# Attention of 64-row halves: score and row products of neighbouring heads in two halves of the array, row sums divided by way of DRAM

## The chip, the cores and the metric

The kernel runs on one core of a Trainium2 chip. The metric is the device time of one execution in microseconds. The profiler's trace of one execution gives the rows that are quoted below. Engines are named as in the profile: PE is TensorE (PEld its weight loads), DVE VectorE, ACT ScalarE, POOL GpSimd, SP SyncE, which here only issues DMAs.

## What is computed

The kernel is a two-layer network on a (2, 1024, 256) input. Each layer holds one causal softmax attention with 16 heads of 16 channels; between and behind them stand expert layers, a frequency mixing and a recurrent layer, which the change does not touch. The attention, cut from the reference:

```python
q = (x @ wq).reshape(b, t, HEADS, HEAD_DIM)     # HEADS 16, HEAD_DIM 16, t 1024
k = (x @ wk).reshape(b, t, HEADS, HEAD_DIM)
v = (x @ wv).reshape(b, t, HEADS, HEAD_DIM)
scores = jnp.einsum('bqhd,bkhd->bhqk', q, k)
mask = jnp.arange(t)[:, None] < jnp.arange(t)[None, :]
scores = jnp.where(mask, -jnp.inf, scores)
attn = jax.nn.softmax(scores / np.sqrt(HEAD_DIM), axis=-1)
ctx = jnp.einsum('bhqk,bkhd->bqhd', attn, v).reshape(b, t, EMB)
return ctx @ wo + bo
```

## The kernel before

`attention` (L343) runs twice, the first time from 39.3 us, the second from 1717 us of the span. It takes the 16 heads of both batch entries in 8 groups of four heads (GH = 4), each group in one **turn**. A turn n works on two groups at once. For group m = n + 1 it makes the **row products** (`first`, L519): 48 matmuls that multiply 128 queries by up to 512 keys, so that VectorE (`maximum`, L672) can take each query's largest score. For group n it makes the **scores** (`scores`, L543), this time with keys in rows and 512 queries in columns; two more contraction rows carry the negated maximum, so that ScalarE (`probabilities`, L633) can go straight from PSUM through the exponential into `a_prob`. Then `values` (L559) multiplies the probabilities by the values, four heads side by side in four 32-column parts of the array. Queries and keys are split in a high and a low part in fp32r, and three of the four products of parts are stacked in the contraction, which is why one head pair takes 96 rows (98 with the maximum).

The function `turn` (L293) writes the order by hand, and all engines follow the same list. A turn has 12 **steps** (STEPS): step i takes one block of 128 keys for one half of the queries, and has four scores, one for each head. Steps 0 to 3 and 8 to 11 lie on the causal diagonal. Their scores are 512, 384, 256 and 128 columns wide, and POOL first cuts a triangle out of the probabilities (L475); steps 4 to 7 are 512 wide and are not cut. `FIRSTS_AFTER` says how many row products follow each score, and the values of step i - 1 come after the four scores of step i. `SMALL` puts one small piece at the end of a step: a projection of queries and keys (`qk`, two a turn, behind steps 3 and 4), one of values (`v`, two a turn), the transposed maxima (`max`, L527), and the division by the row sums (`sums` L568 and `spread` L578 on PE, `reciprocals` L701 and `divide` L706 on DVE), twice a turn. The last turn, the closing one, has no row products and has the output projections (`out`, L591) instead.

Eight PSUM banks hold all this: three for row products (FR = 3), three for scores, one shared by the small pieces (SB = 1), one for the values' sums. An instruction waits for a semaphore count: score t waits until the exponential of score t - SR is done, with SR the number of score banks; a row product waits for the maximum that frees its bank. PE takes its instructions in order, so all that stands behind a waiting matmul waits with it.

```python
if t >= SR:
    pe.wait_ge(s["b_exp"], t - SR + 1)                 # scores, L543
if j == 0 and n * HALF + h:
    pe.wait_ge(s["o_cp"], n * HALF + h)                # values, L559
```

The queries and keys of a head pair reach their rows by DMAs that SP issues (`place_keys`, `place_queries`; for the very first half ScalarE issues them, L620). Each layer's semaphores are cleared by `end_layer`, which also holds a barrier.

## Time and profile before

| | us |
|---|---|
| median of 3 runs (lowest, highest) | 2411.98 (2408.28, 2419.59) |
| profiled execution, its own time | 2414.42 |
| span of that execution | 2412.6 |
| first attention, from the first projection to the last addition | 39.3 to 451.9 |
| second attention | 1717.0 to 2130.9 |
| PE busy over the span | 2034.7 (84%) |
| DVE busy, ACT busy | 1599.6, 856.7 |
| mean granted TensorE clock, share of full speed | 0.908 |

The profiled execution lies 2.4 us above the median. The two attentions are 34% of the span. The stretches of the first one stand in the rows below: start of the projections, row products of the first group alone, first turn, and so on to the closing turn. Busy time is a union of the records of an engine; TensorE's matmuls are pipelined, so that its busy share says only that it was never without one. What one matmul costs its successor is read from start to start.

### The profile page before, as it was taken

The numbers are of one execution on the slowest core, as the hardware profiler recorded it, in microseconds if no ns is written. First come the engines' busy times: TensorE is split into PE (matmuls) and PEld (weight loads), VectorE is DVE, ScalarE is ACT, GpSimd is POOL, SyncE is SP. The second block draws the span as 40 slices with busy tenths as digits, with TensorE's granted clock in tenths as the row PEclk, the third lists the DMA queues.
The fourth block names the chain that finished last, engine by engine and source line by source line (L and its number), as shares of the span: only waits on it lengthen the run. The fifth ranks groups of instructions, "written<-read, shape, count | busy, mean of one in ns | idle before, by whom it ended". The sixth has DMA issues, their size and how long they took to land. (4 is left out here: it accounts for less than half of the span.)

```text
span 2412.6 us, 32196 instructions
## 1 busy us (share of the span) xinstructions
PE 2034.7 (84%) x11288; PEld 1386.3 (57%) x11288; DVE 1599.6 (66%) x3514; ACT 856.7 (36%) x1599; POOL 446.7 (19%) x324
## 2 busy tenths in 40 slices
PE   7899999699999989757766385646689999999998
PEld 4466665388888867334433242323356666469997
DVE  3677773254544355779999999995567777246775
ACT  2255554122223222431112111111335555435775
POOL 0011110423333030001001100110001010105775
PEclk9699999799999999878887698868879999989999
DMA  4111110211110010200000000000121211018886
GB/s 158 42 36 38 44 35 10 83 57 53 52 52 17 0 53 1 86 1 9 9 3 7 18 9 9 0 0 18 36 47 35 47 36 29 9 37 255 235 234 125
DMA packets 52448, 122.19 MB, mean 51 GB/s; under 512 B 14224, under 2 KB 25232, under 8 KB 49488
## 3 DMA queue, kind: packets, MB, share of 16 engines
q1 hardware_dynamic: 42704, 107.40, 14.9%
q0 software_dynamic: 8832, 12.16, 2.9%
q8 instruction: 81, 1.33, 0.2%
q10 hardware_dynamic: 768, 0.79, 0.1%
q14 instruction: 63, 0.52, 0.1%
HBM read 84.09 MB, written 10.52 MB: 39 GB/s over the span
## 5 line engine op out<-in xcount | busy, mean ns | idle before, releaser
L672 DVE CUSTOM_DVE_ANT_0 a_junk<-pair,a_mask 128x512 f32<-128x512 f32 (+3 forms) x768 | 394.2, 551 | 188.1 <-PE pair L519 184.5
L633 ACT ACTIVATE a_prob<-pair 128x512 f32<-128x512 f32 (+3 forms) x768 | 329.0, 496 | 306.5 <-PE pair L543 303.4
L543 PE MATMUL pair<-a_qx,a_kx 98*128 98x512 f32 (+3 forms) x768 | 266.0, 393 | 6.8 <-ACT a_prob L633 6.7
L519 PE MATMUL pair<-a_kx,a_qx 96*128 96x512 f32 (+3 forms) x768 | 246.2, 391 | 22.7 <-DMA a_qx<-a_comp 17.9
L475 POOL TENSOR_SCALAR_AFFINE_SELECT a_prob<-a_prob 128x512 f32<-128x512 f32 x128 | 81.2, 635 | 700.2 <-ACT a_prob L633 700.2
L903 DVE TENSOR_TENSOR m_h<-pair,m_g 128x512 f32<-128x512 f32 x96 | 66.3, 691 | 211.3 <-PE pair L726 210.2
L1285 PE MATMUL pair<-h_stream,r_w_kz 128*128 128x512 f32 x192 | 103.9, 695 | 118.5 <-DVE r_region L1691 113.3
L724 PE MATMUL pair<-m_x_hi,m_w_lo 128*128 128x512 f32 x448 | 178.1, 398 | 26.5 <-POOL m_w_lo L788 24.4
L519 PEld LDWEIGHTS pair<-a_kx,a_qx 96*128 96x128 f32 x768 | 150.6, 204 | 70.4 <-DVE a_mx_raw L672 28.2
L543 PEld LDWEIGHTS pair<-a_qx,a_kx 98*128 98x128 f32 x768 | 143.0, 193 | 74.4 <-ACT a_prob L633 39.3
L725 PE MATMUL pair<-m_x_hi,m_w_hi 128*128 128x512 f32 x448 | 176.8, 395 | 0.0
L726 PE MATMUL pair<-m_x_lo,m_w_hi 128*128 128x512 f32 x448 | 176.8, 395 | 0.0
L559 PE MATMUL pair<-a_prob,a_v 128*32 128x512 f32 (+3 forms) x1536 | 165.4, 503 | 1.5 <-POOL a_prob L475 1.2
L864 ACT ACTIVATE m_g<-pair 128x512 f32<-128x512 f32 x96 | 57.4, 598 | 285.8 <-PE pair L726 285.8
L1329 PE MATMUL pair<-r_hq,r_spread 128*128 128x256 f32 x320 | 86.3, 437 | 84.1 <-DVE r_region L1820 71.4
L1285 PEld LDWEIGHTS pair<-h_stream,r_w_kz 128*128 128x128 f32 x192 | 41.1, 224 | 172.7 <-DVE r_region L1691 116.5
L1705 DVE TENSOR_TENSOR r_region<-r_region 128x1536 f32<-128x1536 f32 (+7 forms) x160 | 129.9, 853 | 2.7
L1345 PE MATMUL pair<-r_u,r_w_ring 128*128 128x512 f32 x256 | 124.0, 630 | 4.8 <-DVE x_stream L1807 4.8
L1329 PEld LDWEIGHTS pair<-r_hq,r_spread 128*128 128x128 f32 x320 | 70.5, 223 | 99.8 <-DVE r_region L1820 74.2
L881 DVE TENSOR_TENSOR m_h_lo<-m_h,m_h_hi 128x512 fp32r<-128x512 f32 x112 | 124.6, 1113 | 0.3
L1555 POOL TENSOR_TENSOR r_y<-r_region 128x512 f32<-128x512 f32 x16 | 20.3, 1269 | 519.7 <-DVE r_region L1820 497.8
L724 PEld LDWEIGHTS pair<-m_x_hi,m_w_lo 128*128 128x128 f32 x448 | 85.5, 191 | 49.8 <-POOL m_w_lo L788 21.5
(305 smaller groups left out, 4254.7 us busy)
## 6 DMA issues: line engine op xcount, KB each, us to landing
mx_raw<-in_L_ffn_experts SPq DMA_DIRECT2D x69, 512.0 KB, 4.9
m_raw<-in_L_cond_experts SPq DMA_DIRECT2D x18, 1024.0 KB, 4.8
a_kx<-a_comp SPq DMA_DIRECT2D x96, 128.0 KB, 2.4
a_qx<-a_comp SPq DMA_DIRECT2D x360, 32.0 KB, 2.0
r_w_ring<-in_r_q_w SPq DMA_DIRECT2D x8, 512.0 KB, 3.9
m_raw<-in_L_cond_experts SPq DMA_DIRECT2D x6, 512.0 KB, 3.4
token_rows<-mx_h_rows SPq DMA_DIRECT2D x2, 1040.0 KB, 8.1
x_stream<-in_x SPq DMA_DIRECT2D x1, 2048.0 KB, 10.6
```

What stands on the lines that cost most here:

```text
L519: nc.tensor.matmul(first_bank[t % FR][:, 0:c1 - c0], qx[0:PRODUCT, m % 2, a, i * P:(i + 1) * P], kx[0:PRODUCT, m % 3, a // 2, c0:c1], star ...
L543: nc.tensor.matmul(score_bank[t % SR][:, q0:TT], kx[0:ROWS, n % 3, a // 2, j * P:(j + 1) * P], qx[0:ROWS, n % 2, a, h * TT + q0:(h + 1) * ...
L559: last = nc.tensor.matmul(value_bank[r, q0:TT], v_sb[:, n % 2, j, r], prob[:, i % RING, a, q0:TT], start=j == 0, stop=j == 4 * h + 3)
L633: nc.scalar.activation(prob[:, i % RING, a, q0:TT], score_bank[t % SR][:, q0:TT], ACT.Exp, scale=SCALE).then_inc(s["b_exp"], 1)
L672: nc.vector.tensor_tensor_reduce(out=junk[:, t % 2, 0:cols], in0=first_bank[t % FR][:, 0:cols], in1=mask[:, m0:m0 + cols], scale=1.0, scal ...
L724: nc.tensor.matmul(out, w_lo, x_hi, start=first, stop=False)
L725: nc.tensor.matmul(out, w_hi, x_hi, start=False, stop=False)
L726: return nc.tensor.matmul(out, w_hi, x_lo, start=False, stop=last)
L881: nc.vector.tensor_tensor(h_lo[:, n % RING, :], h_sb[:, n % 2, :], h_hi[:, n % RING, :].bitcast(F32), ALU.subtract).then_inc(q["lo"], 1)
L1285: last = nc.tensor.matmul(bank, w_kz[:, k, part * DI + m * P:part * DI + (m + 1) * P], seq(c.h, b)[:, k, half(h)], start=k == 0, stop=k == ...
L1329: last = nc.tensor.matmul(spread_bank(v, h)[:, t * QW_:(t + 1) * QW_], spread[:, 2 * h + t, m, :], hq[:, b, v, :], start=True, stop=True)
L1705: did(tt(pr[:, i, :, :, :], right[:, 3 * i:3 * i + 2, :].unsqueeze(1).broadcast_to([P, 3, 2, n]), left.rearrange("p (j q) n -> p q j n", j ...
```

## The change

**Row halves.** A head now takes 48 contraction rows (50 with the maximum) and even heads lie in rows 0 to 63 of the array, odd heads in rows 64 to 127. Row product and score of a slot lie in different halves (`FIRST` now runs over heads 1, 0, 3, 2), so that one can run beside the other. **Banks.** Row products have four PSUM banks, scores two. The maximum writes its masked scores back in place, not to a junk tile. **Order.** One row product follows each score; the values of step i - 1 come after the second score of step i, no longer after the fourth. **Projections.** ScalarE copies the high part twice more (`twin`), so that one DMA places all three parts of a head: 4 DMAs in place of 12 for a half of the queries, and 4 in place of 6 for the keys. Values are projected for two groups at once, once a turn. ScalarE takes over from VectorE the copies of values and of maxima. **Division.** For groups 0 to 6 the PE pieces `sums` and `spread` fall away. The sums go to DRAM, come back as 64 rows, are inverted, go to DRAM again and come back spread over 32 rows for each head; one 1024-column product on DVE divides. The last group keeps the old way. **Layer end.** One more `end_layer` stands ahead of the last branch.

On PE, at step 5 of a middle turn (the L543/L585 rows are scores, L519/L560 row products, L559/L601 values, L494/L533 projections). Before, from the last score of step 4 on:

```order
L543 MATMUL pair<-a_qx,a_kx 128x512 [waits a0_b_exp]
L559 MATMUL pair<-a_prob,a_v 32x128 [waits a0_b_cut,a0_b_exp]
L559 MATMUL pair<-a_prob,a_v 32x128 x3
L494 MATMUL pair<-h_stream,w_qkv 128x512 [waits a0_used]
L494 MATMUL pair<-h_stream,w_qkv 128x512
L543 MATMUL pair<-a_qx,a_kx 128x512 [waits a0_b_exp]
L519 MATMUL pair<-a_kx,a_qx 128x384 [waits a0_a_max]
L543 MATMUL pair<-a_qx,a_kx 128x512 [waits a0_b_exp] x2
L519 MATMUL pair<-a_kx,a_qx 128x512 [waits a0_a_max] x3
L543 MATMUL pair<-a_qx,a_kx 128x512 [waits a0_b_exp]
L559 MATMUL pair<-a_prob,a_v 32x512 [waits a0_o_cp,a0_b_exp]
L559 MATMUL pair<-a_prob,a_v 32x512 x3
```

And now, from the last two scores of step 4 on:

```order
L585 MATMUL pair<-a_qx,a_kx 128x512 [waits a0_b_exp]
L560 MATMUL pair<-a_kx,a_qx 128x512 [waits a0_a_max]
L585 MATMUL pair<-a_qx,a_kx 128x512 [waits a0_b_exp]
L560 MATMUL pair<-a_kx,a_qx 128x512 [waits a0_a_max]
L533 MATMUL pair<-h_stream,w_qkv 128x512 [waits a0_used]
L533 MATMUL pair<-h_stream,w_qkv 128x512
L585 MATMUL pair<-a_qx,a_kx 128x512 [waits a0_b_exp]
L560 MATMUL pair<-a_kx,a_qx 128x128 [waits a0_a_max]
L585 MATMUL pair<-a_qx,a_kx 128x512 [waits a0_b_exp]
L560 MATMUL pair<-a_kx,a_qx 128x128 [waits a0_a_max]
L601 MATMUL pair<-a_prob,a_v 32x512 [waits a0_o_cp,a0_b_exp]
L601 MATMUL pair<-a_prob,a_v 32x512 x3
```

The values of step 4 (the row that waits for `o_cp`) stood behind four scores of step 5 and now stand behind two, and each score waits for the exponential two scores back, not three.

On ACT, at the same place. Before, with the projections' high part (L609), the exponentials (L633) and the copy of the results (L640):

```order
L633 ACTIVATE a_prob<-pair 128x128 [waits a0_b_mm] x3
L609 ACTIVATE a_comp<-pair 128x512 [waits a0_q_in0,a0_q_in1,a0_k_in,a0_proj]
L633 ACTIVATE a_prob<-pair 128x512 [waits a0_b_mm,a0_pv]
L633 ACTIVATE a_prob<-pair 128x512 [waits a0_b_mm] x3
L609 ACTIVATE a_comp<-pair 128x512 [waits a0_proj]
L633 ACTIVATE a_prob<-pair 128x512 [waits a0_b_mm,a0_pv]
L640 ACTIVATE a_o_raw<-pair 128x512 [waits a0_used,a0_pv]
L633 ACTIVATE a_prob<-pair 128x512 [waits a0_b_mm] x3
```

And now, with the high part (L653), the new copies (L655), the exponentials (L690) and the copy of the results (L695):

```order
L690 ACTIVATE a_prob<-pair 128x128 [waits a0_b_mm] x3
L653 ACTIVATE a_comp<-pair 128x512 [waits a0_q_in0,a0_q_in1,a0_k_in,a0_proj]
L655 ACTIVATE a_comp<-a_comp 128x2x512 [waits a0_hi]
L690 ACTIVATE a_prob<-pair 128x512 [waits a0_b_mm,a0_pv]
L690 ACTIVATE a_prob<-pair 128x512 [waits a0_b_mm] x3
L653 ACTIVATE a_comp<-pair 128x512 [waits a0_proj]
L655 ACTIVATE a_comp<-a_comp 128x2x512 [waits a0_hi]
L690 ACTIVATE a_prob<-pair 128x512 [waits a0_b_mm,a0_pv]
L695 ACTIVATE a_o_all<-pair 128x512 [waits a0_pv]
L690 ACTIVATE a_prob<-pair 128x512 [waits a0_b_mm] x3
```

Behind each high part one copy has come in, ahead of the four exponentials of the step.

The diff, cut to its core:

```diff
-PRODUCT = 3 * 2 * HD
+PRODUCT = 3 * HD
...
-FIRST = [(a, i, c_) for part in (range(4), range(4, QT)) for a in range(GH) for i in part for c_ in range(i // 4 + 1)]
+FIRST = [(a, i, c_) for part in (range(4), range(4, QT)) for i in part for c_ in range(i // 4 + 1) for a in (1, 0, 3, 2)]
...
-FR, SB = 3, 1
+FR, SB = 4, 1
...
+SMALL = (("max", 0, 1), None, None, ("qk", 2, 0), ("qk", 2, 1), ("max", 1, 0), ("v", 0, 0), None, None, None, None, None)
...
+NORM = {2: 0, 3: 1, 6: 2, 7: 3, 9: 4}
+NORM_LAST = {1: 0, 2: 1, 4: 2, 5: 3, 6: 4, 8: 5}
...
-            if (i, a) == (0, 1) and n:
-                order += [("values", n - 1, NS - 1), ("copy", n - 1, 1)]
-            for f in range(found, found if closing else min(NF, found + FIRSTS_AFTER[i][a])):
-                order.append(("first", m, f))
+            if (i, a) == (2, 0) and n > 1:
+                order.append(("norm", n - 2, 5))
+            if not closing:
+                order.append(("first", m, found))
                 found += 1
...
+            if a == 1 and i:
+                order.append(("values", n, i - 1))
+            elif a == 1 and n:
+                order += [("values", n - 1, NS - 1), ("copy", n - 1, 1)]
             if (i, a) == (5, 0):
                 order.append(("copy", n, 0))
-        if i:
-            order.append(("values", n, i - 1))
...
+        def rows_of(a, n):
+            return slice(a % 2 * 64, a % 2 * 64 + n)
...
+                    for a in range(GH):
+                        rows = slice(64 + a * HD, 64 + a * HD + HD)
+                        sp.dma_start(kx[rows_of(a, PRODUCT), m % 3, a // 2, :].bitcast(F32), comp[rows, 0:3, :].bitcast(F32))\
+                            .then_inc(s["k_in"], 16)
...
+                    if step == 0:
+                        sp.wait_ge(s["o_cp"], (n + 1) * HALF)
+                        sp.dma_start(totals[n, :, :], o_all[HD:P:SLOT, group, :].rearrange("p h t -> p (h t)"))\
+                            .then_inc(s["n_out"], 16)
+                    elif step == 1:
+                        sp.wait_ge(s["n_out"], (n + 1) * 16)
...
+                        sp.dma_start(total[:, :, :], totals[n, :, :].rearrange("a (p c) -> p a c", p=64)).then_inc(s["n_in"], 16)
...
+                    r = rows_of(a, PRODUCT)
+                    nc.tensor.matmul(first_bank[t % FR][:, 0:c1 - c0], qx[r, m % 3, a // 2, i * P:(i + 1) * P],
+                                     kx[r, m % 3, a // 2, c0:c1], start=True, stop=True).then_inc(s["a_mm"], 1)
...
+                    r = rows_of(a, ROWS)
+                    nc.tensor.matmul(score_bank[t % SR][:, q0:TT], kx[r, n % 3, a // 2, j * P:(j + 1) * P],
+                                     qx[r, n % 3, a // 2, h * TT + q0:(h + 1) * TT], start=True, stop=True)\
                         .then_inc(s["b_mm"], 1)
...
                     nc.scalar.activation(comp[:, 0, half(h)], bank_of("qk", m, h), ACT.Copy).then_inc(s["hi"], 1)
+                    act.wait_ge(s["hi"], m * HALF + h + 1)
+                    nc.scalar.activation(comp[:, 2:4, half(h)], comp[:, 0:1, half(h)].bitcast(F32).broadcast_to([P, 2, TT]), ACT.Copy)\
+                        .then_inc(s["twin"], 1)
...
+                    elif step == 5:
+                        dve.wait_ge(s["n_wide"], (n + 1) * GH * 16)
+                        tile = o_all[:, n * HALF:(n + 1) * HALF, :].rearrange("p h t -> p (h t)")
+                        nc.vector.tensor_tensor(tile, tile, factor[:, :], ALU.mult).then_inc(s["n_done"], 1)
...
         recurrent(c, A)
+        c.end_layer()
```

## Rows read from the trace of the kernel before

**Rows 1.** the page: busy time and share of each engine; granted TensorE clock in 40 slices

```profile
PE 2034.7 (84%) x11288; PEld 1386.3 (57%) x11288; DVE 1599.6 (66%) x3514; ACT 856.7 (36%) x1599; POOL 446.7 (19%) x324
...
PEclk9699999799999999878887698868879999989999
```

**Rows 2.** stretches of the first attention; the first row names the columns

```profile
core 0: us, PE busy (x) PEld busy (x) DVE busy (x) ACT busy (x) POOL busy (x), PEclk, DMA share, GB/s
39.30:57.90 18.60, 10.53 (x41) 6.71 (x41) 5.88 (x8) 3.75 (x4) 4.50 (x6) 0.82 0.45 103
57.90:89.50 31.60, 27.81 (x60) 14.70 (x61) 24.79 (x98) 4.13 (x4) 0.00 (x0) 0.63 0.15 35
89.50:137.70 48.20, 42.62 (x274) 26.43 (x272) 30.14 (x114) 22.30 (x51) 5.08 (x8) 0.85 0.18 41
137.70:178.80 41.10, 41.10 (x325) 26.27 (x321) 29.64 (x112) 22.27 (x52) 5.08 (x8) 1.00 0.18 41
343.20:381.60 38.40, 37.96 (x317) 24.64 (x313) 28.37 (x110) 21.40 (x50) 5.08 (x8) 1.00 0.10 27
381.60:451.90 70.30, 62.49 (x344) 29.98 (x340) 10.39 (x18) 21.40 (x51) 5.08 (x8) 0.93 0.00 1
```

**Rows 3.** groups of TensorE by shape, one middle turn (178.75 to 219.98 us)

```profile
L543 PE MATMUL pair<-a_qx,a_kx 98*128 98x512 f32 x24 | 9.8, 456 | 0.0
L503 PE MATMUL pair<-w_qkv,h_stream 128*128 128x128 f32 x32 | 4.1, 281 | 0.0
L494 PE MATMUL pair<-h_stream,w_qkv 128*128 128x512 f32 x8 | 4.0, 618 | 0.0
L578 PE MATMUL pair<-ident,a_o_rcp 128*32 128x128 f32 x68 | 2.4, 273 | 0.0
L568 PE MATMUL pair<-sum_pick,a_o_raw 128*128 128x4 f32 x16 | 2.1, 255 | 0.0
```

**Rows 4.** groups of ScalarE in the same turn

```profile
L633 ACT ACTIVATE a_prob<-pair 128x512 f32<-128x512 f32 x24 | 12.8, 606 | 7.3 <-PE pair L543 7.3
L609 ACT ACTIVATE a_comp<-pair 128x512 fp32r<-128x512 f32 x2 | 1.2, 598 | 3.9 <-PE pair L494 3.9
```

**Rows 5.** order of time in the closing turn (start, duration, idle before)

```profile
408.88 1.06 PE L559 MATMUL pair<-a_prob,a_v 128*32 128x512 f32 x8
409.87 1.05 PE L568 MATMUL pair<-sum_pick,a_o_raw 128*128 128x4 f32 x8
410.79 0.94 PE L543 MATMUL pair<-a_qx,a_kx 98*128 98x512 f32 x3
411.36 2.06 ACT L633 ACTIVATE a_prob<-pair 128x512 f32<-128x512 f32 x4 [1.49 <-PE pair L543]
412.01 0.50 PE L543 MATMUL pair<-a_qx,a_kx 98*128 98x512 f32 x1 [0.28 <-ACT a_prob L633]
412.44 1.06 PE L559 MATMUL pair<-a_prob,a_v 128*32 128x512 f32 x8
```

**Rows 6.** the same view at that turn's end, narrower steps and the cut

```profile
420.97 1.64 ACT L633 ACTIVATE a_prob<-pair 128x384 f32<-128x384 f32 x4 [3.99 <-PE pair L543]
432.19 0.97 ACT L633 ACTIVATE a_prob<-pair 128x128 f32<-128x128 f32 x4 [4.15 <-PE pair L543]
...
433.23 0.63 POOL L475 TENSOR_SCALAR_AFFINE_SELECT a_prob<-a_prob 128x512 f32<-128x512 f32 x1 [4.49 <-ACT a_prob L633]
434.01 0.43 PE L559 MATMUL pair<-a_prob,a_v 128*32 128x128 f32 x8 [0.59 <-POOL a_prob L475]
```

**Rows 7.** groups of the whole span: 1024-column operations between SBUF tiles

```profile
L2270 ACT ACTIVATE mx_w_hi<-mx_raw 128x1024 fp32r<-128x1024 f32 x69 | 70.3, 1052 | 2.7 <-DMA mx_raw<-in_L_ffn_experts 2.7
L1781 DVE TENSOR_TENSOR r_y<-r_y,r_z 128x1024 f32<-128x1024 f32 x8 | 9.8, 1219 | 1.3 <-ACT r_y L1493 1.3
```

**Rows 8.** order of time: the first attention's start; after the one layer end

```profile
47.66 7.64 ACTq L620 DMA_DIRECT2D a_qx<-a_comp  x12
...
966.63 0.10 DVE L1825 MEMSET r_region<- 128x16 f32 x2 [1.35 <-PEq L56]
```

More of the change, by code:

```diff
@@ L310, in turn @@
                 uses = []
+            if a == 1 and i:
+                order.append(("values", n, i - 1))
+            elif a == 1 and n:
+                order += [("values", n - 1, NS - 1), ("copy", n - 1, 1)]
             if (i, a) == (5, 0):
                 order.append(("copy", n, 0))
-        if i:
-            order.append(("values", n, i - 1))
+        norm = (NORM_LAST if closing else NORM).get(i)
+        if n and norm is not None:
+            order.append(("norm", n - 1, norm))
         small = (SMALL_LAST if closing else SMALL)[i]
@@ L317, in turn @@
             what, x, y = small
-            entry = (what, x, y) if what == "out" else (what, n + x, y)
-            if 0 <= entry[1] < NG:
+            if what == "out":
+                entry = (what, x, y)
+            elif what == "v":
+                entry = (what, n // 2 + 1, n % 2)
+            else:
+                entry = (what, n + x, y)
+            if entry[1] < (NG // 2 if what == "v" else NG):
                 order.append(entry)
@@ L414, in place_keys @@
                     sp.wait_ge(s["used"], used("qk", m, 1))
-                    if m >= 3:
+                    sp.wait_ge(s["twin"], (m + 1) * HALF)
+                    if m < 3:
+                        sp.wait_ge(s["ones"], m + 1)
+                    else:
                         sp.wait_ge(s["b_exp"], (m - 2) * NS * GH)
-                    for p in range(PAIRS):
-                        rows = slice(64 + p * 32, 96 + p * 32)
-                        for part, low in enumerate((0, 1, 0)):
-                            sp.dma_start(kx[part * 32:part * 32 + 32, m % 3, p, :].bitcast(F32), comp[rows, low, :].bitcast(F32))\
-                                .then_inc(s["k_in"], 16)
+                    for a in range(GH):
+                        rows = slice(64 + a * HD, 64 + a * HD + HD)
+                        sp.dma_start(kx[rows_of(a, PRODUCT), m % 3, a // 2, :].bitcast(F32), comp[rows, 0:3, :].bitcast(F32))\
+                            .then_inc(s["k_in"], 16)
                 def place_queries(m, h):
@@ L439, in place_maxima @@
                 def place_maxima(m, h):
                     sp.wait_ge(s["used"], used("max", m, h))
[L441 to L442 removed]
+                    for x in range(2):
+                        sp.dma_start(qx[x * 64 + PRODUCT:x * 64 + ROWS, m % 3, :, half(h)].bitcast(F32),
+                                     stage[2 * PAIRS * x:2 * PAIRS * x + 2 * PAIRS, :].bitcast(F32))\
@@ L460, in _ @@
             def _(pool):
-                for a in range(GH):
-                    nc.gpsimd.memset(qx[:, 1, a, :].bitcast(F32), 0.0).then_inc(s["zero1"], 1)
+                for x in range(3):
+                    nc.gpsimd.memset(kx[:, x, :, :].bitcast(F32), 1.0).then_inc(s["ones"], 1)
                 nc.gpsimd.memset(v_sb[:, :, :, :].rearrange("p x t (a s) -> p (x t a) s", s=SLOT)[:, :, HD:HD + 1], 1.0)\
@@ L496, in qk_projection, with v_projection @@
                     last.then_inc(s["proj"], 1)
-                def v_projection(m, v):
-                    bank = take("v", m, v)
+                def v_projection(pair, v):
+                    m = 2 * pair
+                    bank = take("v", pair, v)
                     for t in range(4):
@@ L613, in place_first_queries @@
                         return
[L614 removed]
                     act.wait_ge(s["used"], used("qk", 0, 0))
+                    act.wait_ge(s["twin"], 1)
                     for a in range(GH):
                         rows = slice(a * HD, a * HD + HD)
[L618 to L625 removed]
+                        act.dma_start(qx[rows_of(a, PRODUCT), 0, a // 2, half(0)].bitcast(F32), comp[rows, 1:4, half(0)].bitcast(F32))\
+                            .then_inc(s["q_in0"], 16)
                 def probabilities(n, i, a):
@@ L637, in copy_result @@
                     act.wait_ge(s["pv"], n * NS + (4 if h == 0 else NS))
-                    if n:
-                        act.wait_ge(s["used"], used("spread", n - 1, h))
-                    nc.scalar.activation(o_raw[:, h, :], value_bank, ACT.Copy).then_inc(s["o_cp"], 1)
-                does = {"qk": upper, "q_slots": place_first_queries, "scores": probabilities, "copy": copy_result}
+                    nc.scalar.activation(o_all[:, n * HALF + h, :], value_bank, ACT.Copy).then_inc(s["o_cp"], 1)
+                does = {"qk": upper, "q_slots": place_first_queries, "scores": probabilities, "copy": copy_result,
+                        "v_use": copy_values, "max_use": copy_maxima}
                 for what, *which in ORDER:
@@ L648, in _ @@
             def _(dve):
-                for a in range(GH):
-                    nc.vector.memset(qx[:, 0, a, :].bitcast(F32), 0.0).then_inc(s["zero0"], 1)
                 dve.wait_ge(s["mask"], 16)
```

170 lines of the change are left out of this document (87 added, 83 removed).

## Prediction

> **What bounds the kernel now.** The page comes first: PE is busy 84% of the span, in the attentions 99% [rows 1]. The stretches say more [rows 2]: a middle turn takes 41.1 us and PE is busy in all of it at full clock, while DVE has 29.6 us and ACT 22.3 us of work. The groups of that turn show no idle time ahead of any PE group, and ACT idle for want of scores (7.3 us) and of projections (3.9 us) [rows 3, 4]. So a middle turn is TensorE's time. What that leaves unseen is the latency around ACT, since PE always has something else to do. The closing turn, which has no row products, shows it [rows 5]: the fourth score waits for a bank (idle 0.28, released by ACT).
>
> **TensorE's work after the change.** Three 512-column scores start 0.24 us apart (0.94 [rows 5] less one duration of 0.46 [rows 3], halved). A turn has 24 such scores and 24 narrower ones (by width about 0.12 each), some 8.6 us, and as many row products. If the halves run side by side, half of 17.2 is saved, 8.6. The sums and the spread go (2.1 + 2.4), and half of the value projections (4.1 / 2 = 2.0) [rows 3]. That is 15.1 us, and 26.0 remain of 41.1. The Trainium skill (TensorEngine Tiling (Array Packing), Theoretical Speedup) gives up to 2x for a contraction of 64 or less; no row here shows row halves, and by that rule the saving would be this 8.6. Its section PSUM Bottleneck speaks against the change: tiling speeds up TensorE and not the emptying of PSUM.
>
> **What is late next: the round through ACT with two banks.** Handovers from [rows 5]: a first score starts at 410.79 and its exponential at 411.36, 0.57 later. Four exponentials take 2.06, one 0.61, so each follows the last by 0.48. The waiting score starts at 412.01, 1.22 after the first, and the values 0.43 later; from values to the next PE work it is 0.99 (408.88 to 409.87). The cut comes from [rows 6]: POOL starts 0.07 after the last exponential (its row 432.19 + 0.97 = 433.16), takes 0.63, and the values start at 434.01: 0.85 in all.
>
> Now one step in the new order, from the start of its third score (time 0). A 512-wide step without cut: third exponential 0.57 to 1.18, fourth to 1.66. The first score of the next step needs the third's bank, 1.2; the second needs the fourth's, 1.7. Row products run beside them. The values follow the second: 1.7 + 0.43 + 0.1 for the row product = 2.2, and the next third score starts at 3.2. PE has about 2.0 us of work in it, ACT 1.9. With the cut, the values start at 1.66 + 0.85 = 2.5, the next third score at 3.5. For narrower steps exponentials take 0.37 apart at 384 columns, about 0.27 at 256 and 0.17 at 128 (1.64 and 0.97 for four [rows 6]), and values shrink by 0.21 per 128 columns (1.06 against 0.43 busy [rows 5, 6]): 3.1, 2.6 and 2.1. Without extras a turn is 2 x (3.5 + 3.1 + 2.6 + 2.1) + 4 x 3.2 = 35.4 us.
>
> **The projections inside this round.** The high part and the new copy stand ahead of the exponentials on ACT. Two projections are busy 4.0 us, one 2.0 [rows 3], the high part 0.6 [rows 4], the copy 1.05 (1024 columns [rows 7]). From the third score of step 3: projection 0.6 to 2.6, high part to 3.2, copy to 4.3, two exponentials to 5.35; the third score of step 4 waits for the first of them, 4.9, its fourth exponential ends at 6.5. The second projection goes in at 5.7, ends 7.7, high part 8.3, copy 9.35, exponential 9.9, result copy 10.4. The values of step 4 wait for that result copy (`o_cp`), 10.5, so the third score of step 5 starts at 11.5. Without the projections it is 2.1 + 3.2 = 5.3: +6.2. Value projection behind step 6: 16 matmuls at half of 4.1 less the overlap, +0.9. The result copy at the turn's start +0.3; two copies of the maxima (0.6 each) fit in ACT's idle time. Turn: 35.4 + 6.2 + 0.9 + 0.3 = **42.8 us, 1.7 more than now**. I take this and keep -2 and +2.5 us a turn as bounds: 0.2 us a step if the first score after the values needs less than the 0.57 seen, as much if the row product delays them.
>
> **The other parts.** DVE loses sums, spread product, value and maxima copies and gains one 1024-column product of 1.2 us [rows 7] and a reciprocal, staying under 29.6 us: hidden as long as the turn is over that. In-place masking into PSUM has no row; 0, within 0.06 us of a maximum either way, and only the first 48 maxima feel it. The DRAM trips: five steps on SP and DVE over a turn, the product one turn later still; a DMA issue takes 0.64 us (12 in 7.64 [rows 8]), and a step lasts 2 us or more. SP's queue holds `place_keys` and `place_maxima` behind these waits, needed 6 to 20 us later: 0. If a trip took over 8 us, DVE would stop at its reciprocal with all maxima behind it. Start of an attention: now 18.6 + 31.6 us [rows 2]. The 12 issues on ACT become 4, saving 5 us of the 7.64, and two copies and the values' copies give half back: -2.5. The 48 maxima need 24.8 of 31.6 us; fourth bank and halves give -2.5. Bounds of both together 0 and -9. Turn 6 has no projections: 35.4 + 0.3 + 0.7 (result copy ahead of the values of step 4) = 36.4 against 38.4, -2. Closing turn: the same outputs, one pair of sums and spread fewer, longer rounds: 0, bounds -3 and +3. The layer end: DVE stood 1.35 us at the first one [rows 8]; +1.
>
> **The sum.** Per attention: turns 0 to 5 at +1.7 = +10.2, start -5, turn 6 -2, closing 0: +3. Two attentions and the layer end: 2 x 3.2 + 1 = +7.4 on the profiled 2414.4. The median lies 2.4 lower: 2412 + 7.4 = **2420 us**. The bounds of the turn (12 x -2 and +2.5, not both full with the others) give 2392 to 2450. A measurement of this kernel tells 0.5% (12 us) from no change.
>
> **Rival 1, slower: the clock.** TensorE's granted clock is 1.00 (2.4 GHz) in the middle turns, where PE never pauses, and 0.63 where it waited for DVE between row products [rows 2], that is mostly the 1.2 GHz level. The new turn pauses 17 of 42.8 us, up to 2.5 us at a time around the second projection. The first turn shows the price: granted 0.85, 48.2 against 41.1, +7.1 us [rows 2]. All 12 turns from 0 to 5 at 0.85 give about 12 x 7 = +85 on the 2420: 2505. Above 1 us a turn it decides the sign. Against it: the closing turn pauses too and keeps 0.93. The Trainium skill (TensorE: Matmul & The Clock Gate, psum-queue depth-cycling) tells of a kernel whose short pauses between groups made the clock oscillate, and would side with this rival.
>
> **Rival 2, faster: the round is shorter than its parts.** The score after the values starts loaded (0.3, not 0.57) and the values end 0.3 us sooner for the next score. That is 0.55 us a step, 6.6 a turn: 36.2, 12 x 6.6 = 79 less, 2341. Half of it gives 2380. For it: the 0.57 has a weight load in it. Against: the 1.22 and 0.99 repeat in each step of the closing turn.
>
> **Rival 3: the halves don't run side by side.** Then each row product costs 0.24 us where it stands ahead of values or projection, some 6 places: +1.5 a turn, 2440. That TensorE's 15 us would simply be gained (turn at DVE's 27 to 29 us, near 2260) I hold for hardly possible, since the bank wait is in the code.
>
> **Chances.** Forecast with its own range 0.45, clock 0.27, shorter round 0.23, no concurrency 0.05. Of the forecast 0.08 lies under 2400, 0.20 within 12 us, 0.17 above; rival 2 gives 0.22 to faster. Faster 0.30, same 0.21, slower 0.49. The range runs from 2350, halfway down rival 2, to 2520, just above the clock at 0.85; 0.1 on each side is left out.
>
> **What would show it.** Right: middle turns of 41 to 45 us; PE idle with ACT as the releaser of scores, POOL and ACT of values; the longest hole ahead of the values that follow the second projection; ACT idle still some 15 us a turn. Rival 1: granted clock under 0.95 in turns 1 to 6. Rival 2: turns under 40 us with PE still idle. Rival 3: row product and score starting 0.24 us apart, not together. Wrong altogether: DVE waiting at the reciprocal for a DMA, or DVE busy over 30 us a turn.

## Result and the profile after

The changed kernel takes 2533.4 us (median of 4), the kernel before 2411.4 beside it: ratio 1.050, 95% interval 1.047 to 1.054, 122 us slower. That lies above the range of the prediction, and 113 us above its point.

The profiled execution lasts 2537.9 us against 2412.6. The page's engine shares and granted clock, to be held against [rows 1]:

```profile
PE 2061.3 (81%) x9912; PEld 1246.9 (49%) x9912; DVE 1601.2 (63%) x3414; ACT 921.6 (36%) x1689; POOL 453.7 (18%) x322
...
PEclk9577777889999999888888698778677877698999
```

TensorE has 1376 products fewer and is busy 27 us longer. Both attentions stand mostly at 7 or 8 tenths of the clock where the kernel before had mostly 9. The stretches of the first attention (stretch, length, busy time of each engine with its instructions, granted clock, DMA share and GB/s), answering [rows 2]. The first two are its start, then turn 0, turn 2, four pieces from the start of turn 4 (295.3 to 345.5) on, turn 6 and the closing turn:

```profile
core 0: us, PE busy (x) PEld busy (x) DVE busy (x) ACT busy (x) POOL busy (x), PEclk, DMA share, GB/s
37.50:55.80 18.30, 9.69 (x40) 5.42 (x40) 1.38 (x2) 4.62 (x8) 7.15 (x5) 0.91 0.43 92
55.80:88.40 32.60, 27.92 (x60) 13.82 (x61) 24.53 (x93) 3.89 (x5) 0.00 (x0) 0.57 0.20 38
88.40:141.40 53.00, 44.34 (x217) 17.03 (x216) 29.79 (x106) 26.42 (x56) 4.44 (x7) 0.72 0.24 43
192.90:243.00 50.10, 42.08 (x224) 17.38 (x224) 30.48 (x107) 27.13 (x59) 5.98 (x8) 0.76 0.23 44
295.60:312.60 17.00, 15.08 (x71) 6.15 (x69) 10.83 (x42) 7.48 (x18) 3.89 (x5) 0.50 0.02 4
312.70:322.90 10.20, 6.66 (x38) 2.29 (x36) 4.54 (x14) 6.82 (x11) 0.00 (x0) 1.00 0.11 13
322.90:329.70 6.80, 6.74 (x31) 3.32 (x29) 3.81 (x13) 3.71 (x7) 0.00 (x0) 0.51 0.79 154
329.70:346.80 17.10, 14.20 (x104) 5.91 (x103) 12.24 (x41) 9.89 (x24) 2.54 (x4) 1.00 0.24 56
397.50:440.70 43.20, 36.97 (x200) 13.86 (x200) 28.88 (x106) 23.44 (x53) 5.99 (x8) 0.68 0.09 27
440.70:511.50 70.80, 63.15 (x296) 27.39 (x297) 11.78 (x23) 23.12 (x53) 5.71 (x9) 0.83 0.04 9
```

A middle turn takes 48.9 to 52.2 us where it took 41.1 (the mean of turns 1 to 5 of both attentions is 50.96). Within turn 4 the granted clock goes between its two levels: 0.50 (1.2 GHz) from the turn's start to its fourth step, up to 1.00 (2.4 GHz), once more down, and at 1.00 in steps 7 to 11. The other middle turns have the same 1.00 in steps 7 to 11 and the fall behind it. Measured from the first score of each turn to that of the next, turns 0 to 5 give +55.3 us in the first attention and +54.3 in the second, the two turns 6 give +4.9 and +10.2, all else +0.6. That is the 125.3 us between the two spans. So it is the turns, and nearly nothing but the turns.

What TensorE waits for in turn 2 (busy, mean, then the idle time ahead and who ended it), and the longest hole of turn 4 in the order of time:

```profile
L585 PE MATMUL pair<-a_qx,a_kx 50*128 50x512 f32 (+3 forms) x48 | 20.2, 489 | 3.5 <-ACT a_prob L690 3.5
L601 PE MATMUL pair<-a_prob,a_v 128*32 128x512 f32 (+3 forms) x96 | 13.3, 632 | 4.5 <-ACT a_o_all L695 2.3 <-POOL a_prob L514 1.7 <-ACT a_prob L690 0.5
```

```profile
310.41 3.15 PE L533 MATMUL pair<-h_stream,w_qkv 128*128 128x512 f32 x4
...
316.74 1.98 PE L533 MATMUL pair<-h_stream,w_qkv 128*128 128x512 f32 x4
318.65 0.50 PE L585 MATMUL pair<-a_qx,a_kx 50*128 50x512 f32 x1
318.66 0.32 PE L560 MATMUL pair<-a_kx,a_qx 48*128 48x128 f32 x1
...
321.56 1.07 PE L601 MATMUL pair<-a_prob,a_v 128*32 128x512 f32 x8 [2.30 <-ACT a_o_all L695]
```

L585 is the score, L560 the row product, L601 the values, L533 a projection, L690 the exponential, L695 the result copy, L514 POOL's cut. TensorE had no idle time at all in [rows 3]; now scores wait for exponentials and values for the result copy and the cut. A score and the row product of the other half start 0.01 us apart (318.65, 318.66). The same four projection products last 1.98 us at the upper level of the clock (316.74), 3.15 where the clock rises while they run (310.41, granted 0.62) and 3.78 at the lower level throughout (at 74.56 us).

### The profile page after: what moved, and what is told of

Its sections match the earlier page's. It is cut to its first block and busy times, and to the rows that moved or that the text cites. A ratio compares the mean times of both kernels' runs of the same rounds, so it can differ in the third digit from the quotient of the medians.

```text
span 2537.9 us, 28385 instructions
## 1 busy us (share of the span) xinstructions
PE 2061.3 (81%) x9912; PEld 1246.9 (49%) x9912; DVE 1601.2 (63%) x3414; ACT 921.6 (36%) x1689; POOL 453.7 (18%) x322
## 5 line engine op out<-in xcount | busy, mean ns | idle before, releaser
L717 DVE CUSTOM_DVE_ANT_0 pair<-pair,a_mask 128x512 f32<-128x512 f32 (+3 forms) x768 | 412.9, 582 | 318.9 <-PE pair L560 317.9
L690 ACT ACTIVATE a_prob<-pair 128x512 f32<-128x512 f32 (+3 forms) x768 | 349.2, 489 | 351.6 <-PE pair L585 342.0
L585 PE MATMUL pair<-a_qx,a_kx 50*128 50x512 f32 (+3 forms) x768 | 320.0, 500 | 50.5 <-ACT a_prob L690 49.5
L560 PE MATMUL pair<-a_kx,a_qx 48*128 48x512 f32 (+3 forms) x768 | 327.7, 524 | 9.6 <-DMA a_kx<-a_comp 4.2
L585 PEld LDWEIGHTS pair<-a_qx,a_kx 50*128 50x128 f32 x768 | 155.6, 231 | 338.2 <-ACT a_prob L690 208.4
L601 PE MATMUL pair<-a_prob,a_v 128*32 128x512 f32 (+3 forms) x1536 | 217.3, 644 | 64.4 <-ACT a_o_all L695 31.9
L514 POOL TENSOR_SCALAR_AFFINE_SELECT a_prob<-a_prob 128x512 f32<-128x512 f32 x128 | 90.3, 705 | 816.5 <-ACT a_prob L690 816.5
L560 PEld LDWEIGHTS pair<-a_kx,a_qx 48*128 48x128 f32 x768 | 160.3, 239 | 32.7 <-DVE a_mx_raw L717 21.2
L533 PE MATMUL pair<-h_stream,w_qkv 128*128 128x512 f32 x128 | 103.8, 957 | 15.1 <-DVE a_comp L709 10.5
```

The costliest lines, as they stand in the source:

```text
L560: nc.tensor.matmul(first_bank[t % FR][:, 0:c1 - c0], qx[r, m % 3, a // 2, i * P:(i + 1) * P], kx[r, m % 3, a // 2, c0:c1], start=True, sto ...
L585: nc.tensor.matmul(score_bank[t % SR][:, q0:TT], kx[r, n % 3, a // 2, j * P:(j + 1) * P], qx[r, n % 3, a // 2, h * TT + q0:(h + 1) * TT], ...
L601: last = nc.tensor.matmul(value_bank[r, q0:TT], v_sb[:, n % 4, j, r], prob[:, i % RING, a, q0:TT], start=j == 0, stop=j == 4 * h + 3)
L690: nc.scalar.activation(prob[:, i % RING, a, q0:TT], score_bank[t % SR][:, q0:TT], ACT.Exp, scale=SCALE).then_inc(s["b_exp"], 1)
L717: nc.vector.tensor_tensor_reduce(out=first_bank[t % FR][:, 0:cols], in0=first_bank[t % FR][:, 0:cols], in1=mask[:, m0:m0 + cols], scale=1. ...
```

## Experiments

Times are medians beside runs of the kernel before (2411 to 2415 us). "Clock" is the granted clock of a stretch. In the two theories most of them tell apart, **round** says that a turn is the chain score, exponential, next score over the banks, with the projections and copies in it; **clock** says that the pauses let TensorE's clock fall and that this is most of the loss. "The combination" is the kernel of experiment 8.

**1. More work for TensorE: 43 idle four-byte products a turn** (128 columns, into the shared bank while it is free).

```
+ if not closing and (a or not pending): order.append(("fill",))
+ nc.tensor.matmul(shared_bank[0][:, 0:128], c.ident[:, :], c.h[:, 0, 0:128], start=True, stop=True)
```

> The changed kernel, with an idle product of 128 columns put behind nearly every row product of turns 0 to 6 (some 46 a turn, 0.21 us each at full clock, 10 us a turn); nothing reads what it writes into the free shared bank. Theory clock (TensorE's pauses cost mainly by the granted clock that falls in them): the granted clock of a middle turn rises from 0.74 to over 0.9 and turns get shorter although there is more work, from 51 to 43 to 46 us, the total near 2440 to 2480. Theory round (the turn is the round through the two score banks, at whatever clock): the clock may rise, but turns stay at 50 to 55 us and the total at 2530 to 2590.

2720.5 us, from 2681.9 to 2754.5; the trace is of the shortest. The turns are not shorter, but the clock follows the filler: in turns 2 and 4 it is 1.00, over turns 1 to 5 of both attentions 0.93 in the mean (0.84 to 1.00). Turns 1 and 2, and the filler's row in turn 2 (two passes each):

```profile
153.70:215.50 61.80, 58.05 (x312) 29.76 (x311) 31.80 (x105) 28.51 (x58) 5.13 (x9) 0.89 0.18 36
215.50:272.00 56.50, 52.03 (x312) 26.73 (x310) 32.56 (x106) 28.51 (x58) 5.93 (x8) 1.00 0.20 39
...
L651 PE MATMUL pair<-h_stream,ident 128*128 128x128 f32 x88 | 21.5, 326 | 1.0 <-DVE a_comp L719 0.8 <-ACT a_v L671 0.2
```

Equal instructions differ by 5.3 us between 0.89 and 1.00. Steps 7 to 11 of turn 4, at 1.00 in both kernels, take 20.59 us with the filler and 14.63 without: 19 pieces, 0.31 us each, all of it on the path and not the 0.21 I had put. Taking 43 x 0.314 = 13.5 off the 56.6 leaves 43.1: an estimate of the changed kernel's turn at full clock. It takes the price of a piece to be the same in the other steps. Where the changed kernel runs those at or near full clock (steps 0, 4 and 5: 2.68, 5.16 and 5.09 us, against 3.98, 5.76 and 6.26 with the filler) a piece costs 0.2 to 0.4 us, 0.31 in the mean, so that 43.1 may be off by about 1 us. The expectation for "clock" misjudged what the filler costs; its first half, the clock over 0.9, came true in the mean and in six of the ten turns.

**2. One-pass filler** (the same places, a product of the identity table, 128 columns).

> As the kernel with idle products, but each a one-pass product of 128 columns of the identity table, estimated at a third of the time of the four-byte one (which cost 0.30 us a piece at full clock). Theory clock: what matters is whether TensorE stays in use; if this filler is enough, turns are at 1.00 and 43.2 plus 44 times 0.1, 45 to 48 us, total 2460 to 2500, less than the changed kernel with more work. If it is not enough, clock 0.75 to 0.85 and the filler's time is added: 2550 to 2600.

2771.9 us, clock 0.68 in turn 2, turns of 62 to 70 us. Not only too little: the clock is lower than with none, for which I have no cause that the runs show. A filler isn't harmless because it is short.

**3. Three score banks, three for row products** (`FR, SB = 3, 1`).

> The changed kernel with the banks split as in the kernel before, three for row products and three for scores. Theory round: with a third score bank a score waits for the exponential three back and not two back, so a 512-column step lasts about 2.4 to 2.7 us at full clock instead of 3.2; turns of 36 to 42 us and a total of 2330 to 2420, and if the pauses shrink the clock rises by itself. Theory clock without a part of the banks in it (the halves alone leave TensorE too little to do): the granted clock stays near 0.75 and turns stay over 46 us, total over 2480.

2480.6 us, 53 less; turns 1 to 5 take 46.3 to 50.2 us at 0.71 to 0.85, mean 47.2. At the edge of the second expectation: the third bank is worth 3.7 us a turn, but the clock stays down.

**4. The bank split alone, in the kernel before.**

```
-FR, SB = 3, 1
+FR, SB = 4, 1
```

> The kernel before with one part of the change alone: four banks for row products and two for scores; no row halves. TensorE has 41 us of serial work in a turn there. Theory round: it stands between one exponential and the next score, so most of the bank wait is covered; turns of 41 to 43 us at a clock of 1.00, total 2411 to 2440. Theory that the two score banks by themselves cost what the third bank gave back in the last comparison (53 us): turns over 44 us, clock under 0.95, total 2455 to 2480.

2493.2 us, 81 slower than before. Turn 1 there:

```profile
139.90:185.70 45.80, 44.02 (x330) 26.03 (x320) 29.89 (x112) 23.66 (x52) 5.08 (x8) 1.00 0.16 36
```

45.8 us for 41.1 at a clock of 1.00, and the same in all ten turns 1 to 5: this part costs 4.7 us a turn without any help of the clock. Neither expectation had that: the second had the turn over 44 us, but at a clock under 0.95 and with a lower total. The waits for a score bank were not covered by 41 us of serial work, and little of the cost shows as idle time. The scores' row of that turn:

```profile
L543 PE MATMUL pair<-a_qx,a_kx 98*128 98x512 f32 (+3 forms) x48 | 19.4, 414 | 1.8 <-ACT a_prob L633 1.6
```

Idle time ahead of scores is 1.8 us; the other 2.9 lie in PE's busy time (44.0 for 41.1). In the closing turn of this run a score that had waited starts together with its weight load (both at 420.34) where one that had not starts 0.07 us behind it (419.18, 419.25), so such loads may be part of the 2.9; how much wasn't measured.

**5. Row products in the order of heads 0 to 3**, each in the half of the score ahead of it.

```
-for a in (1, 0, 3, 2)]
+for a in (0, 1, 2, 3)]
```

> The changed kernel with the row products in the order of heads 0, 1, 2, 3, so that each falls into the same row half as the score before it and cannot run beside it. Theory round: the halves side by side bring nearly nothing where TensorE waits anyway; turns grow by the 0.24 us of a row product at some 6 to 12 places, 51 to 54 us, total 2540 to 2570. Theory clock: TensorE is in use for some 8 us more of each turn, which may keep its clock up; then the clock rises above 0.8 and turns are at most as long as now, total 2480 to 2533.

2538.9 us, 1.0508 of the kernel before where the changed kernel has 1.0504: no clear difference. But the order does not take the concurrency away, as the expectation supposed. The score of the next head lies in the other half, and now two scores start together and then two row products (step 2 of turn 2, at the lower level of the clock):

```profile
208.79 0.59 PE L585 MATMUL pair<-a_qx,a_kx 50*128 50x256 f32 x2
209.17 0.53 PE L560 MATMUL pair<-a_kx,a_qx 48*128 48x384 f32 x2
```

Counted over both attentions, 768 of the 1536 scores and row products start within 0.025 us of another one here, 1000 in the changed kernel and none in the kernel before. So this run compares two ways of pairing; what the halves side by side are worth was not measured.

**6. The result copy ahead of the second projection's high part and twin copy on ScalarE.**

```
-            if (i, a) == (5, 0):
+            if (i, a) == (4, 3):
                 order.append(("copy", n, 0))
```

> The changed kernel with the copy of the first half's result at the end of step 4 on ScalarE, ahead of the second projection's high part and twin copy, instead of behind the first exponential of step 5. The forecast's step (the values of step 4 wait for this copy behind a projection's two operations): the 2.3 us hole of TensorE ahead of those values closes to under 1 us, a turn loses 1.5 to 2.3 us, total 2505 to 2518. If the hole is only passed on to the next wait (the exponential of step 5 behind the same two operations): under 0.5 us a turn, total 2527 to 2535.

2493.9 us, 40 less, more than expected. The values' idle time in turn 2 no longer names the result copy:

```profile
L601 PE MATMUL pair<-a_prob,a_v 128*32 128x512 f32 (+3 forms) x96 | 12.4, 594 | 2.4 <-POOL a_prob L514 1.9 <-ACT a_prob L690 0.5
```

Steps 5 and 6 of turn 1 fall from 6.01 and 6.15 us to 3.57 and 4.59, 4.0 us for a hole of 2.3: the clock comes back sooner behind it (0.73 to 0.78 over the turn).

**7. No twin copy** (DMAs read the high part twice). In this kernel and in the first combination below the query rows of a head stand in another order than its key rows, so other products are summed; the work is the same.

```
-nc.scalar.activation(comp[:, 2:4, half(h)], comp[:, 0:1, half(h)].broadcast_to([P, 2, TT]), ACT.Copy)
```

> The changed kernel without ScalarE's 1024-column twin copy behind each projection's high part (1.06 us, two a turn); the DMAs read the high part twice instead, 24 issues a turn on the DMA queue of SyncE in place of 12. Theory that each operation ahead of the exponentials lengthens the round: a turn loses 2 to 3 us, total 2495 to 2512, and the clock rises a little. Theory that ScalarE has slack there: 2525 to 2535. If the doubled issues make the maxima's or the queries' rows late: slower than 2533.

2473.4 us, 60 less, where 21 to 38 was expected by the first theory: 5.5 us a turn for 2.1 us of copies, again with the clock (0.81 to 0.85).

**8. The three together.**

> The changed kernel with three score banks (53 us less by itself), the early result copy (40 us less by itself) and no twin copy. If the three holes are separate: 2533 less 53, 40 and some 30 is 2410. Theory clock: with the holes closed TensorE keeps 2.4 GHz, turns fall to 36 to 39 us and the total to 2350 to 2390, under the kernel before. If TensorE has too little work for its clock even so, the granted clock stays under 0.9, turns at 42 to 45 us and the total at 2415 to 2450.

2436.0 us. Singly they gave 53 + 40 + 60 = 153, together 97. The expectation for "too little work" holds: turns of 42.5 to 43.8. With the rows in matching order it is 2436.5:

> The changed kernel with three score banks, the early result copy and no twin copy, and the query rows in the order that matches the key rows (in the two earlier kernels without the twin copy the row products paired other rows, a change in what is computed and not in the work). Every theory expects the time of the earlier combination, 2430 to 2442, and its turns of 42.5 to 43.8 us at a granted clock of 0.76 to 0.88.

**9. The combination, with the row products in the order of heads 0 to 3.**

> The combination, with the row products in the order of heads 0 to 3, so that none runs beside a score (some 8 us more of serial work for TensorE in a turn). Theory clock: with the other waits gone this work is enough to keep 2.4 GHz; turns of 37 to 40 us at 0.95 or more, total 2360 to 2400, less than with the halves side by side. Theory that the clock only follows the waits for ScalarE and POOL: it stays at 0.75 to 0.85 and turns grow by 1 to 3 us, total 2445 to 2475.

2446.8 us, 10 more, clock 0.77 in most turns. As in experiment 5 the products still pair, 914 of 1536 for 920 in the combination, so that the 10 us are the price of the other order and not the worth of the concurrency.

**10. VectorE's 1024-column product at step 5 instead of step 2**, in the changed kernel and in the combination. In the changed kernel, turn 4:

```profile
303.00 1.22 DVE L757 TENSOR_TENSOR a_o_all<-a_o_all,a_factor 128x1024 f32<-128x1024 f32 x1
303.17 1.54 POOL L514 TENSOR_SCALAR_AFFINE_SELECT a_prob<-a_prob 128x512 f32<-128x512 f32 x1 [3.78 <-ACT a_prob L690]
...
304.86 1.46 PE L601 MATMUL pair<-a_prob,a_v 128*32 128x384 f32 x5 [1.01 <-POOL a_prob L514]
```

```
-            if (i, a) == (2, 0) and n > 1:
+            if (i, a) == ((2, 0) if closing else (5, 0)) and n > 1:
                 order.append(("norm", n - 2, 5))
```

> The changed kernel with nothing but VectorE's 1024-column product moved from step 2 to step 5. In the combination the move gave 14 us. Theory that POOL's cut and the values behind it carry over: 1 to 1.5 us a turn here too, total 2515 to 2522. Theory that the round through ScalarE hides a slow cut: 2528 to 2536.

> The combination, with VectorE's 1024-column product at step 5, in which POOL cuts nothing, and not at step 2. Theory that the product slows POOL's cut beside it (1.54 us where others take 0.63) and the values wait for that cut: the 1 us hole ahead of the values of step 1 or 2 goes, 0.8 to 1.5 us a turn, total 2418 to 2428. If the cut is slow for another reason: no difference, 2430 to 2442.

Alone 2539.2 us, no gain (1.0526 of before, interval 1.051 to 1.054, against 1.0504, 1.047 to 1.054). In the combination 2422.3, 14 less. Turn 2 of it and turn 3, the same instructions, and the cut's group in turn 2:

```profile
173.30:212.70 39.40, 35.76 (x228) 15.73 (x228) 30.11 (x107) 23.86 (x57) 5.10 (x8) 0.93 0.30 58
212.70:255.20 42.50, 39.45 (x226) 17.49 (x225) 29.41 (x104) 23.87 (x56) 5.10 (x8) 0.79 0.26 50
...
L517 POOL TENSOR_SCALAR_AFFINE_SELECT a_prob<-a_prob 128x512 f32<-128x512 f32 x8 | 5.1, 637 | 33.3 <-ACT a_prob L693 33.3
```

The cut is back at 637 ns a piece. POOL's cut took 1.54 us beside the product and 0.63 without it. The Trainium skill (GPSIMD Engine Reference, Key points) says that POOL shares its SBUF interfaces with VectorE and contends with VectorE instructions that have two SBUF inputs, as this product has; the trace agrees, the difference being 0.9 us. A hole that was 1 us long was worth nothing while others followed it, and 1.2 us a turn once they were gone, part of it by the clock (0.83 for 0.80 in the mean of turns 1 to 5).

**11. The place of the values**: behind the fourth score of the next step in the changed kernel, behind the third in the combination with the moved product (`if a == 2 and i:` for `a == 1`).

> The changed kernel with the value products of a step behind the fourth score of the next step instead of the second, near where the kernel before has them. Theory that the place of the values costs in the change (they wait for the fourth exponential, the cut and the result copy with the next scores queued behind them): the 2.3 us hole and the cut's wait are covered, 2 to 4 us a turn, total 2480 to 2510. If the two score banks already hold the scores back: under 1 us a turn, total 2520 to 2540.

> The combination with the moved product, and the value products behind the third score of the next step instead of the second. TensorE's hole ahead of the values (0.7 us behind POOL's cut at full clock) would be covered by one more score. Theory waits: 0.3 to 0.6 us in each of the 5 to 8 steps with a cut, turns of 36 to 39 us, total 2375 to 2410, under the kernel before. If the exponentials' ring or VectorE (29.5 us a turn) is the next limit: 2410 to 2425. If the lighter stretches let the clock fall more often: over 2425.

With two score banks and the fourth score it is 2599.4 us, 66 more, against both expectations: with two banks the place that the change chose is the better one. With three banks and the third score it is 2401.5, 21 less than without, ratio to before 0.9959 (0.9945 to 0.9973); turns of 40.4 to 41.5 at 0.79 to 0.83, where the theory of the waits had 36 to 39.

**12. Where the rest of the clock goes.** Eight four-byte idle products a turn in steps 0 to 3 of the combination of 8 (`i < 4 and a in (1, 3)`); the three projections spread over other steps (two kernels, from 2401.5); and the eight idle products in steps 8 to 11 (`i > 7`, also from 2401.5).

> The combination, with the four-byte idle product of 128 columns twice in each of steps 0 to 3 (8 a turn, 0.30 us each at full clock) instead of 44 a turn; the granted clock falls from step 2 or 3 on. Theory that the quiet steps ahead of the fall decide it: the clock stays at 1.00, turns of 38 to 41 us, total 2370 to 2410. If eight are too few: clock unchanged and up to 2.4 us more a turn, total 2440 to 2470.

> The best combination so far (2401 us), with the projections put where TensorE has least to do: queries and keys behind steps 1 and 3 instead of 3 and 4, the values' behind step 9 instead of 6. Theory clock: the granted clock falls in steps 2 to 4 after the quiet narrow steps; with work spread evenly it stays over 0.95 and a turn takes 36 to 38 us, total 2350 to 2375. If the order of the same work does not matter to the clock: 2395 to 2410.

> As the one beside it, with the projections behind steps 2 and 4 and the values' behind step 8. Theory clock: between the best so far and the one with steps 1, 3 and 9, 2360 to 2395. If the order does not matter: 2395 to 2410.

> The best combination (2401 us) with the four-byte idle product of 128 columns twice in each of steps 8 to 11, the stretch just ahead of the place where the granted clock falls to the 1.2 GHz level (it is down in steps 0 to 4 of a turn). TensorE waits 0.7 to 0.9 us in each of those steps, so that the 0.3 us a piece are nearly hidden. Theory clock, with the quiet steps ahead of the fall deciding it: granted clock over 0.95, turns of 36.5 to 38.5 us, total 2350 to 2375. If the amount of work over the turn decides it, or the pauses of steps 0 to 4 themselves: clock 0.80 to 0.88 as before, total 2395 to 2415.

Fills in steps 0 to 3: 2465.6, 29 more; the clock rises a little (0.85 for 0.80 in the mean of turns 1 to 5), which doesn't pay for the pieces. The run holds the cleanest price of the clock, two turns of one kernel:

```profile
1843.70:1884.00 40.30, 36.73 (x244) 17.47 (x243) 29.27 (x106) 24.06 (x57) 5.10 (x8) 0.97 0.26 49
1884.00:1931.00 47.00, 43.35 (x243) 20.31 (x242) 30.11 (x105) 24.16 (x57) 6.00 (x8) 0.79 0.25 46
```

6.7 us between 0.97 and 0.79. Spreading the projections gave 2409.1 and 2424.9 where 2350 to 2395 was expected: turns alternate between 39.3 us at 0.91 and 42.7 at 0.84 in the first, so the order of the same work shifts the clock's falls but doesn't end them. I had read the fall as lying in steps 2 to 4; the stretches above put it at a turn's start, behind the quiet steps 7 to 11. The last run tries that place:

2394.9 us, ratio 0.9917 (0.990 to 0.9935), with more work than the kernel at 2401.5. Its turns 2 and 3, and turn 3 of the kernel without the fills:

```profile
173.90:214.60 40.70, 38.95 (x241) 17.78 (x242) 30.27 (x107) 24.11 (x57) 5.10 (x8) 0.92 0.29 54
214.60:252.40 37.80, 36.00 (x241) 16.90 (x241) 30.06 (x107) 23.95 (x57) 5.10 (x8) 1.00 0.31 58
```

```profile
215.60:255.90 40.30, 38.71 (x225) 17.26 (x224) 29.64 (x106) 23.96 (x56) 5.10 (x8) 0.83 0.29 53
```

Odd turns of the first attention (1, 3, 5) are at 1.00 and 37.8 us, even ones at 0.92; the second attention has some at 0.84 and 42.8. The forecast of 2350 to 2375 needed 1.00 in all. It is the fastest kernel of the study, 0.8% under the kernel before.

## Why the prediction was wrong

**The step that failed** is the level of the clock in the forecast. All its terms were read at 2.4 GHz and the turn of 42.8 us was put together from them, though the same text counted 17 us of pauses a turn. At full clock the turn was nearly right: about 43.1 by the estimate of experiment 1. The measured 50.96 (granted 0.75) are 7.9 us more, and by that estimate this is the clock. The waits give 43.1 less 41.1, 2.0 a turn, for a forecast of 1.7.

**TensorE's work, -15.1 us.** The halves do run side by side, so that rival 3 is out. Two pairs of 512-column products start 0.34 us apart at full clock (313.50 and 313.84), where two such products one behind the other take 0.47 in the kernel before (0.23 to 0.24 each): a pair saves 0.13 us there, and the forecast had 0.24. (In experiment 4 a single score that had waited often stands 0.34 us ahead of the next product too, so that a weight load may be part of the pair's 0.34.) But what leaves the work of an engine that then waits is mostly not gained. With the bank split alone the turn is 45.8 us at full clock, with the whole change some 43.1: halves, order, projections and division together give back 2.7 us. How much of that is the halves no run shows, since none took the concurrency away.

**The round through ScalarE.** Step for step right where the clock is 1.00: from the third score of step 7 of turn 4 on, the periods are 3.34 for the last uncut step and 3.47, 2.98, 2.50 and 2.08 for the cut ones, and the forecast had 3.2, 3.5, 3.1, 2.6 and 2.1. Experiment 4 shows that the bank split costs 4.7 us a turn even in the kernel before, with its serial work: what a pause-free TensorE [rows 3] hid was how closely the third score bank was needed.

**Projections inside the round, +6.2.** From the third score of step 3 to that of step 5 the forecast has 11.5 us. In turn 4 it is 309.48 to 322.56, 13.1, of which 1.2 is the first projection, most of it at 1.2 GHz (3.15 for 1.98). The longest hole stands where it was put, 2.30 us ahead of the values behind the second projection, released by the result copy. What moving it gave (40 us, where 15 to 28 was expected) shows again that a hole costs its length and a piece of the clock.

**Rival 1, the clock.** The right mechanism at a chance of 0.27. Its price was taken from the first turn, granted 0.85 and +7.1 us, and some 7.9 came. That the two are near is luck. The 7.1 are mostly not the clock: TensorE is busy 42.6 of that turn's 48.2 us [rows 2], and nearly all the rest is one wait for the queries' DMA:

```profile
95.75 0.77 PE L519 MATMUL pair<-a_kx,a_qx 96*128 96x128 f32 x2 [5.58 <-DMA a_qx<-a_comp]
```

The 1.5 us that are left of the 7.1 are no clean price either, since that turn has fewer products (274 for 325) [rows 2]. The middle turns paid their 7.9 at 0.75, without any such wait. What lifted the time from 2505 to 2533 are the places where the rival was not applied. Turn 6 was put at 36.4 and took 43.2 (granted 0.68) and 48.5 (0.52); the start of an attention was to lose 5 us, and the first took 50.9 for 50.2, at 0.57 in its second stretch where 0.63 stood before. Whether the clock alone made the start miss was not measured. I held the closing turn's 0.93 against the rival; it has heavy output projections that the middle turns lack, and now shows 0.83 itself. The Trainium skill (TensorE: Matmul & The Clock Gate, psum-queue depth-cycling) tells of short pauses between groups of products that make the clock oscillate. The trace agrees: down and up inside nearly every turn. The Trainium skill (same page, Loop structure matters more than you think) names long waits for a DMA as the bad case; here no pause of TensorE in a turn exceeds 2.3 us and the clock falls nevertheless.

**Rival 2** (a shorter round) is out: the steps at full clock have the forecast's length.

**Hidden parts.** Right: DVE never waits at the new reciprocal; it is busy 29.4 to 30.5 us a turn, in some turns just over the 30 that was to mean "wrong altogether", but far under the turn's 50; the trips through DRAM cost nothing; the closing turn of the first attention is 70.8 for 70.3. Masking in place makes a maximum 31 ns longer (582 against 551 in the whole span's groups) and is hidden. Misread: TensorE is busy 99% only in turns 1 to 6; over the whole first attention it is 386.9 of 412.6 us, 94%. Not seen: VectorE's product slows a cut of POOL beside it by 0.9 us, and the values behind it.

**Of the 125 us between the spans**, the ten turns 1 to 5 hold 98.5 (50.96 for 41.11 each): some 79 are the clock by the estimate of experiment 1, some 20 the waits at full clock, each good to about 10. The two turns 0 hold 11, the two turns 6 hold 15, and how much of these is clock wasn't measured. How the 2.0 us of waits a turn divide among banks, copies and cut can't be told by adding, since the single removals overlap.

## What to carry to other kernels

Before taking work off an engine that never waits, ask what it will wait for then: here four scores passing through two banks cost 4.7 us a turn, more than all the rest of the change gave back at full clock (2.7). Where TensorE will pause and did not before, price the turn at both levels of its clock, from two turns of the trace that differ in the clock and in nothing else, and give the fall a high chance. When an experiment is to take a concurrency away, look in its trace whether it is gone: two reordered kernels here kept theirs. A hole removed may give more than its length while the clock is down, and a small idle product can pay if it stands in the quiet steps ahead of the fall, though in most places it costs its full time.

## What the runs showed of the hardware

- With the same instructions a turn took 40.3 us at a granted clock of 0.97 and 47.0 at 0.79; 37.8 at 1.00 and 40.7 at 0.92; 56.5 at 1.00 and 61.8 at 0.89.
- Eight four-byte products of 128 columns in the quiet steps raised the granted clock of a turn from 0.83 to 1.00 or 0.92 in the first attention, and to between 0.84 and 1.00 in the second. Forty-three one-pass products lowered it from 0.76 to 0.68 in turn 2; that isn't explained.
- Two PSUM banks for scores instead of three made a turn 45.8 us instead of 41.1 at a clock of 1.00, with 1.8 us of idle time ahead of the scores.
- A cut of POOL (128x512) took 1.54 us beside a VectorE product with two SBUF inputs of 1024 columns, 0.63 otherwise.
- A product of 48 and one of 50 rows in different halves of the array start 0.01 us apart and both last 0.5 us at 512 columns; the next such pair starts 0.34 us later at full clock. They pair also when the two are not neighbours in program order: with the order score, row product, score, row product in halves 0, 0, 1, 1 the two scores start together.
